# The chunked recurrence of a two-layer network, cut into two halves of eight heads

## The reference, cut to what matters

```python
def step(S, inp):
    qi, ki, vi, ei = inp
    kh = jnp.einsum('bchd,bhde->bche', ki, S)
    target = vi - ki
    mu = jnp.mean(kh, -1, keepdims=True)
    rstd = jax.lax.rsqrt(jnp.var(kh, -1, keepdims=True) + EPS)
    kh_hat = (kh - mu) * rstd
    g = w * kh_hat + b - target
    gw = g * w
    v_new = (gw - jnp.mean(gw, -1, keepdims=True) - kh_hat * jnp.mean(gw * kh_hat, -1, keepdims=True)) * rstd
    A = jnp.einsum('bchd,bshd->bhcs', qi, ki)
    A = jnp.where(tri, A, 0.0) * jnp.transpose(ei, (0, 2, 1))[:, :, None, :]
    qh = jnp.einsum('bchd,bhde->bche', qi, S) - jnp.einsum('bhcs,bshe->bche', A, v_new)
    S = S - jnp.einsum('bchd,bche->bhde', ki * ei[..., None], v_new)
```

## Time and profile before

| what | us |
|---|---|
| median of 3 runs | 2653.61 |
| the profiled execution's own time | 2670.09 |
| its span, first to last instruction | 2668.3 |
| PE busy in the span | 2252.8 (84%) |
| DVE busy in the span | 1594.0 (60%) |
| stretch from the first `u` to the last (865.1 to 1216.9) | 351.80 |

### The profile page before, as it was taken

The page is one execution under the profiler, slowest core; times in us unless marked ns, Lnnn a source line. Parts: engine busy times, 40 slices in busy tenths (PEclk is TensorE's granted clock), DMA queues, the critical chain, the costliest instruction groups (busy, mean ns, idle before and its releaser), DMA issues. The chain is left out here.

```text
span 2668.3 us, 49920 instructions
## 1 busy us (share of the span) xinstructions
PE 2252.8 (84%) x19076; PEld 1951.7 (73%) x19076; DVE 1594.0 (60%) x3469; ACT 1079.2 (40%) x2039; POOL 1037.0 (39%) x809
## 2 busy tenths in 40 slices
PE   8999994689983999994678994999999999999930
PEld 6888884567772898893446773999998999999920
DVE  4665555456551768766957633656655665665658
ACT  3222222266553323323431211555555555555523
POOL 2553542122221000003510475666665666666621
PEclk9999996799996878866999996999999999999965
DMA  2101102245546536524520002234235523333147
GB/s 107 37 25 37 36 21 92 86 166 186 191 173 220 126 92 174 139 49 132 177 105 12 1 2 94 68 136 140 74 136 197 202 82 136 106 110 130 40 177 279
DMA packets 154536, 299.96 MB, mean 112 GB/s; under 512 B 66841, under 2 KB 93209, under 8 KB 139645
## 3 DMA queue, kind: packets, MB, share of 16 engines
q1 hardware_dynamic: 108285, 181.82, 21.2%
q0 software_dynamic: 44480, 115.41, 12.9%
q10 hardware_dynamic: 1616, 0.62, 0.1%
HBM read 296.83 MB, written 106.27 MB: 151 GB/s over the span
## 5 line engine op out<-in xcount | busy, mean ns | idle before, releaser
L91 PE MATMUL bank<-routed_xh,routed_guh 128*128 128x256 f32 (+1 forms) x1536 | 438.5, 285 | 27.8 <-DVE routed_xl L2130 27.8
L92 PE MATMUL bank<-routed_xh,routed_gul 128*128 128x256 f32 (+1 forms) x1536 | 438.5, 285 | 0.0
L93 PE MATMUL bank<-routed_xl,routed_guh 128*128 128x256 f32 (+1 forms) x1536 | 436.1, 284 | 0.0
L2164 DVE TENSOR_TENSOR routed_gul<-routed_guf,routed_guh 128x2816 fp32r<-128x2816 f32 x64 | 198.0, 3094 | 250.9 <-ACT routed_guh L2107 250.9
L91 PEld LDWEIGHTS bank<-routed_xh,routed_guh 128*128 128x128 f32 (+1 forms) x1536 | 281.6, 183 | 36.2 <-issue 33.8
L2048 POOL DMA_INDIRECT routed_x<-mid_x,routed_xi x132 | 278.0, 2106 | 55.4 <-issue 52.9
L93 PEld LDWEIGHTS bank<-routed_xl,routed_guh 128*128 128x128 f32 (+1 forms) x1536 | 283.2, 184 | 0.0
L92 PEld LDWEIGHTS bank<-routed_xh,routed_gul 128*128 128x128 f32 (+1 forms) x1536 | 281.2, 183 | 2.0
L2057 POOL DMA_INDIRECT mid_y<-routed_y,routed_yi x132 | 139.2, 1054 | 247.6 <-ACT routed_y L2123 225.1
L2107 ACT CAST routed_guh<-routed_guf 128x2816 fp32r<-128x2816 f32 x64 | 163.4, 2553 | 35.4 <-DMA routed_guf<-in_GU,routed_wi 32.8
L2117 ACT CAST routed_ih<-routed_sil 128x256 fp32r<-128x256 f32 (+1 forms) x192 | 78.0, 406 | 240.6 <-DVE routed_sil L2169 240.6
(11 more groups left out here) (455 smaller groups left out, 5884.9 us busy)
## 6 DMA issues: line engine op xcount, KB each, us to landing
last_y<-mid_y SPq DMA_DIRECT2D x16, 1536.0 KB, 9.8
mid_ks<-ffn_kT SPq DMA_DIRECT2D x16, 1024.0 KB
mid_qs<-ffn_qT SPq DMA_DIRECT2D x16, 1024.0 KB
ttt_KQ<-mid_ks SPq DMA_DIRECT2D x16, 1024.0 KB, 7.2
ttt_KQ<-mid_qs SPq DMA_DIRECT2D x16, 1024.0 KB, 12.6
mid_te<-ffn_te SPq DMA_DIRECT2D x16, 264.0 KB
ttt_te<-mid_te SPq DMA_DIRECT2D x64, 66.0 KB, 5.4
gla_xT<-in_xT SPq DMA_DIRECT2D x16, 256.0 KB, 3.0
```

The source lines that it names most:

```text
L91: pe.matmul(out, hi(c), whi(c), start=start and c == 0, stop=False, skip_group_check=True)
L92: pe.matmul(out, lo(c), whi(c), start=False, stop=False, skip_group_check=True)
L93: last = pe.matmul(out, hi(c), wlo(c), start=False, stop=stop and c == n - 1, skip_group_check=True)
L2164: nc.vector.tensor_tensor(gul[q][:].rearrange("p a c n -> p (a c n)"), guf[q][:], guh[q][:].bitcast(F32).rearrange("p a c n -> p (a c n)") ...
```

## The change

The four groups are split in two halves `h` of GH = 2 groups (eight heads), which share nothing. Every semaphore of the recurrence exists once for each half, and every temporary has its own name, so that no instruction of one half waits for the other half's. Each half has its own PSUM banks for the state, the queries' product, the keys' product and A; KK lies in the bank of the queries' product, behind it. `u` and `ub` have two buffers.

Each engine's program alternates between the halves, half a step apart. On PE a half step is KH, SU and AU of one half, KS and QS of the other, then prep of the first. On DVE the second part of one half's chain stands interleaved with the first part of the other's. ACT does five operations for one half and then five for the other. The copy by sequence (`ub`) stays on DVE but moves behind the first part of the other half. No arithmetic changes; an instruction handles half the columns, and there are twice as many.

```diff
-    bS, bQ, bA, bC = bank[0:4]
-    bH = bank[4:6]
-    G = KC
+    HALVES, G = 2, KC
+    GH = G // HALVES
+    bS, bQ, bH, bA = bank[0:2], bank[2:4], bank[4:6], bank[6:8]
+    AFTER_Q = GH * DH
...
+            def both(n, h, m, k):
+                if (n or h) and n + h < STEPS:
+                    by_sequence(n - 1 + h, 1 - h)
+                to_goal(n, h)
+                rates(n, h)
+                along_keys(n, h)
+                masked(n, h)
+                along_summed(n, h)
+                if m < STEPS:
+                    squares_summed(m, k)
+                projected(n, h)
...
+                update(n, h)
+                if m < STEPS:
+                    weighted_centred(m, k)
+                    inverse(m, k)
+                    keys_normed(m, k)
+                    weighted_normed(m, k)
...
             for n in range(STEPS):
+                for h in range(HALVES):
+                    if n + 1 < STEPS:
+                        deviation(n + 1, h)
+                        state(n + 1, h)
+                    result(n, h)
+                    if n + 2 < STEPS:
+                        next_keys(n + 1, h)
...
             for n in range(STEPS):
-                f, r = place(n)
-                pe.wait_ge(s["S"], n + 1)
...
+                for h in range(HALVES):
+                    pe.wait_ge(done["u"][h], n + 1)
+                    if n + 1 < STEPS:
+                        keys_corrected(n + 1, h)
+                        state_updated(n, h)
+                    queries_corrected(n, h)
+                    m, k = n + h, 1 - h
+                    if m + 1 < STEPS:
+                        keys_times_state(m + 1, k)
+                    if m < STEPS:
+                        queries_times_state(m, k)
+                    if n + 1 < STEPS:
+                        prepare(n + 1, h)
```

More of the change, by code:

```diff
@@ L1215, in state, with deviation @@
[L1215 to L1219, removed]
[L1220 to L1235 removed]
+            def deviation(n, h):
+                act.wait_ge(done["KH"][h], n + 1)
+                nc.scalar.activation(sq[:, heads(h)].rearrange("p g e -> p (g e)"), bH[h][:, 0:GH * DH], ACT.Square).then_inc(done["sq"][h], 1)
+                act.wait_ge(done["s2"][h], n + 1)
+                nc.scalar.activation(sd[:, h], s2[:, h], ACT.Sqrt, scale=1.0 / DH, bias=eps[:, 0:1]).then_inc(done["sd"][h], 1)
@@ L1247, in over_e @@
             def over_e(t):
-                return t.unsqueeze(2).to_broadcast([P, G, DH])
-            for n in range(STEPS):
-                f, r = place(n)
[L1252 to L1265, removed]
+                return t.unsqueeze(2).to_broadcast([P, GH, DH])
@@ L1294, in _ @@
+            first_of(0, 0)
+            for n in range(STEPS):
+                both(n, 0, n, 1)
+                both(n, 1, n + 1, 0)
         @block.tensor
@@ L1313, in keys_times, with of, column, keys_times_state @@
-            def keys_times(out, n, other, made):
-                for g in range(G):
+            def of(h):
+                return range(h * GH, (h + 1) * GH)
+            def column(g, width):
+                return slice(g % GH * width, (g % GH + 1) * width)
+            def keys_times_state(n, h):
+                pe.wait_ge(done["S"][h], max(n, 1))
+                if n:
+                    pe.wait_ge(done["hat"][h], n)
+                for g in of(h):
+                    for b in range(B):
+                        last = pe.matmul(bH[h][half(b), column(g, DH)], keys(n, g, b), S[:, g, b, :],
+                                         start=(g == h * GH), stop=False, skip_group_check=True)
+                last.then_inc(done["KS"][h], 1)
@@ new lines, in keys_corrected, with state_updated @@
+            def keys_corrected(n, h):
+                pe.wait_ge(done["cross"][h], n)
+                for g in of(h):
+                    for b in range(B):
+                        last = pe.matmul(bH[h][half(b), column(g, DH)], cross[half(b), g, :], u[(n - 1) % 2][half(b), g, :],
+                                         start=False, stop=True, skip_group_check=True)
+                last.then_inc(done["KH"][h], 1)
+            def state_updated(n, h):
+                f, r = place(n)
+                pe.wait_ge(done["ub"][h], n + 1)
+                for g in of(h):
+                    last = pe.matmul(bS[h][:, column(g, B * DH)], kk[f][:, r, g].rearrange("p j d -> p (j d)"),
+                                     ub[n % 2][:, g].rearrange("p b e -> p (b e)"), start=False, stop=False, skip_group_check=True)
+                last.then_inc(done["SU"][h], 1)
```

223 lines of the change are left out of this document (134 added, 89 removed).

## The result

The changed kernel takes 2823.19 us (median of 4, 2817.49 to 2829.56), the kernel before 2654.53 (median of 4). The ratio is 1.0607, 95% interval 1.0554 to 1.0659: 6% slower, where 2814 us was forecast.

The account below looks back on a forecast made before the run. PE at half clock throughout was taken as the bound: 7.44 us plus 0.68 us of switches, 8.12 us a step, 63 steps 512 us against 351.8, so 2653.6 + 160 = 2814 us; range 2771 to 2840, 8 in 10 2695 to 2855.

Parts of the forecast that it names:

- Half clock from the first step to the last: Recurrence: PE stays at 1.2 GHz throughout and is the bound, 8.12 us a step, 2814 us in all; chance 0.72.
- the rises come with a long dense run and the new order has none: PE in the recurrence: clock rises stand behind 64 matmuls of prep, KS and QS; the new order has only 32 together.
- a full clock would hold, once there: PE in the recurrence: full clock, if reached, would last, since a half step has only small gaps and prep comes twice.
- 7.44 + 4 x 0.17 = 8.12 us: PE's step at half clock: 7.44 us now plus four more switches of the array's use at 0.17 us each.
- both are hidden: Half clock: DVE's 2.40 us and ACT's 1.45 us a half step lie within PE's 4.06 us.
- DVE's forecast 2.40: DVE in a half step at full rate: its operations take up 2.40 us, so 4.80 us a step.
- the ring: Full clock: the loop sum, root, state copy, result, prep, KH, square, put at 2.3 to 2.6 us a half step.
- +160 us: Recurrence: 63 steps at 8.12 us are 512 us against 351.8, so 160 us more.
- Full clock throughout: Rival for the recurrence: PE's smaller gaps keep the clock up, 4.9 us a step, 2611 us in all; chance 0.15.
- A mixed clock as now: Rival for the recurrence: 40% of the time at half clock, 5.83 us a step, 2669 us in all; chance 0.11.
- The interleaving does take place: Rival denied this: a semaphore still chains the halves, giving DVE gaps; no change at half clock under 4.06 us; no chance given.
- DVE by the length of its operations: Rival for DVE: operations cost full lengths, 7.24 us a step even at full clock, 2758 us in all; chance 0.02.

Follow-up runs that it names:

- b_split: Kernel before, not halved, with the 16 matmuls keys x queries of prep moved between KH and SU; ratio 1.0488 to the kernel before.
- a_burst: Changed kernel with AU ahead of SU, 14 dense matmuls on zeros at the start and 8 every eighth step; 2708.49 us, ratio 1.0225 to the kernel before.
- a_again: Changed kernel with AU ahead of SU and A of each half computed three times; one run, 2793.79 us beside 2742.75 for the kernel before.
- a_fill: Changed kernel with one dense 128x256 matmul on zeros ahead of A in each half step; one run, 2993.82 us.
- a_warm: Changed kernel with 14 dense matmuls on zeros ahead of the second half's first A; ratio 1.0478 to the kernel before.
- a_warm_au: Changed kernel with 14 dense matmuls on zeros at the start and AU ahead of SU; ratio 1.0483 to the kernel before.
- a_au: Changed kernel with AU put ahead of SU in each half step, one switch less; ratio 1.0573 to the kernel before.
- b_fill: Kernel before with one dense 128x256 matmul on zeros behind QS in each step; ratio 0.9963 to the kernel before.
- b_fill5: Kernel before with one dense 128x256 matmul on zeros behind QS in each step, same program as b_fill on another chip; ratio 0.9989 to the kernel before.

## Why the prediction was right

*The clock.* Half clock from the first step to the last was the likeliest case, and it came. The step of the argument that could have failed, that the rises come with a long dense run and the new order has none, is borne out: cutting the run of before leaves no rise (b_split), a dense run put into the halved order lifts the clock each time that it fell (a_burst), and a longer run of its own groups does (a_again). The prediction had read two rises of the kernel before; all 17 bear it out. a_fill fits the expectation but not plainly the argument: its added matmul is wide and dense, and one in each half step lifts nothing. So that the order of PE's groups sets the clock is shown; which property of the run does it is not. That a full clock would hold, once there, is true until a stall.

The prediction asked little about falls, and there the two orders differ. In the kernel before 15 of 17 falls come with no stall, behind the wait for `u`. In the four kernels that run the halved order at full clock for a time (a_warm, a_warm_au, a_burst, a_again) there are ten falls, and each lies in a stall of "issue" or at most 2.6 us behind one; eleven other stalls, of 0.28 to 1.07 us, brought none. In these runs the halved order loses its clock only by a stall, and what it can't do is get it back.

*PE's step.* 7.44 + 4 x 0.17 = 8.12 us was the forecast, 8.13 the mean, 8.17 in the steady state; KH's start-to-start time is 0.57 us, 0.58 was forecast. That it is so close is in part luck. With the 0.14 that a_au shows for a switch, half of 7.44 and two switches give 4.00 us for a half step and not 4.09; 0.05 of what is missing is in KS and QS, which cost 0.87 together where half of the earlier trace rows without a switch is 0.82. And the first step is some 2 us shorter than the others, which lowers the mean.

*DVE and ACT.* At half clock both are hidden, as forecast: no wait of PE for either is left but at the start. DVE waits there more for A (147.3 us, at `am`) than for the square (51.1 us), where I had named the square alone. At full clock a half step is 2.37 us, and that isn't DVE's forecast 2.40: PE has no gap in it but a stall (57.34 of 58.00 us busy from 862 to 920 in a_warm), and with one switch less on PE DVE keeps up with 2.33 (a_warm_au). The prediction had DVE or the ring as the bound there; it is PE. It also read the 27.0 us of PE's waits for `u` as mostly the start, which is 6.33 of them. The forecast used neither.

*The sum.* +160 us was forecast for the stretch and it is +160.7 (512.5 - 351.8). The median moved by 168.7, the profiled execution by 154.7 (2824.83 against 2670.09).

*The rivals.* Full clock throughout would have needed both a dense start and no stall; a_warm had the first and lost the clock after 62 us, and a busy PE didn't bring it in the changed kernel (512.07 of 512.50 us at 0.50). A mixed clock as now needs rises, and there was none. The interleaving does take place: with all instructions a step is 4.75 us in a_warm. DVE by the length of its operations is out: the sum at 1003.09 is 0.22 us long and the next operation starts at 1003.23. The section that the prediction cites against the change, "The DRAIN you can't avoid" in "VectorE: DVE Perf Modes" of the Trainium skill, itself goes on that a next operation which isn't held starts earlier. The prediction left that out, so these rows contradict its reading, not the whole section.

## What to carry to other kernels

Where TensorE runs many small matmuls, read the time of a step at each granted clock apart and ask of a new order first which clock it will get; an order that spreads the dense groups evenly can lose more by the clock than it gains by overlap. Here the overlap worked, but at full clock it gave 4.75 us a step instead of 4.87, and at half clock a step is 8.17. Where TensorE is the bound, a switch between groups that use the array in another way is paid (0.14 us in a_au, 0.21 in b_split), so put groups of one form together. A busy TensorE is no sign that its clock is full.

## What the runs showed of the hardware

The granted clock can stay at either level for the same program: 62 us at 2.4 GHz, then 408 us at 1.2 GHz, with TensorE busy for all of the 408 (a_warm). TensorE at times stands idle in the middle of a group of matmuls with nothing in the profile to wait for, for 0.2 to 3.3 us; in b_fill and b_fill5, one program, at the same matmuls. Some of these stalls are followed by a fall of the clock (0.47 us in a_warm, 2.59 in b_fill5), others aren't (1.07 us in a_again, 1.36 in b_fill). A switch between a use of 64 x 64 of the array and one of 128 x 128 costs 0.14 us at half clock (a_au).
